# Cross attention of a decoder layer: weighings in pairs, other places for the maxima, the closing of the sums moved

## The reference, cut to what matters

```python
scores = jnp.einsum('bhqd,bhkd->bhqk', q, k) / np.sqrt(DK).astype(np.float32)
scores = jnp.where(mask == 0, jnp.float32(-1000000000.0), scores)
attn = jax.nn.softmax(scores, axis=-1)
out = jnp.einsum('bhqk,bhkd->bhqd', attn, v)
```

## Time and profile before

| | us |
|---|---|
| median of 3 runs | 3819.49 (3815.13 to 3820.21) |
| profiled execution | 3817.16 |
| its span, first to last instruction | 3815.3 |
| PE busy in the span | 3730.7 (98%) |
| granted share of PE's clock, mean | 0.993 |

### The profile page before, as it was taken

How to read it: one execution, slowest core, us unless ns; L and a number is a source line. 1 busy time by engine, 2 the same in 40 slices (tenths; PEclk the granted TensorE clock), 3 DMA queues, 4 the chain that set the end, 5 groups by cost and what they waited for, 6 DMA issues and landing times. The chain is left out here.

```text
span 3815.3 us, 62978 instructions
## 1 busy us (share of the span) xinstructions
PE 3730.7 (98%) x18664; PEld 2480.3 (65%) x18665; DVE 2386.6 (63%) x6129; ACT 1434.0 (38%) x1793; POOL 1687.6 (44%) x984
## 2 busy tenths in 40 slices
PE   8999999999988999999999999999999999999998
PEld 7888888788876544444444444454444777777886
DVE  6544444344466888888888888888888543434235
ACT  3222222222333455545555455545555221222332
POOL 2222222200023776677666766676665222312334
PEclk9999999999999999999999999999999999999999
DMA  6444444555565122222211222222211434327679
GB/s 203 125 128 131 134 121 121 162 199 187 180 196 180 36 58 58 58 56 58 58 29 34 58 58 59 58 56 58 48 31 40 157 123 138 111 89 257 213 279 340
DMA packets 245485, 446.75 MB, mean 117 GB/s; under 512 B 20024, under 2 KB 104536, under 8 KB 241244
## 3 DMA queue, kind: packets, MB, share of 16 engines
q1 hardware_dynamic: 215196, 366.37, 33.3%
q0 software_dynamic: 14752, 49.29, 3.6%
q10 hardware_dynamic: 15264, 27.79, 1.9%
HBM read 262.21 MB, written 181.17 MB: 116 GB/s over the span
## 5 line engine op out<-in xcount | busy, mean ns | idle before, releaser
L1165 DVE CUSTOM_DVE_ANT_0 xf_unread<-xa_mx_ps,mask_q 128x402 bf16<-128x402 f32 x1984 | 1033.7, 574 | 279.0 <-PE xa_mx_ps L1158 152.8
L1788 ACT ACTIVATE probs<-xa_scores 128x1024 f32<-128x1024 f32 (+1 forms) x416 | 417.5, 1024 | 417.6 <-PE xa_scores L1662 411.5
L1788 ACT ACTIVATE xa_probs<-xa_scores 128x1024 f32<-128x1024 f32 (+1 forms) x416 | 417.3, 1024 | 387.0 <-PE xa_scores L1662 387.0
L1662 PE MATMUL xa_scores<-mask_t,ident_b 128*128 128x512 bf16 (+1 forms) x1664 | 549.4, 388 | 0.0
L1623 POOL TENSOR_TENSOR xa_sums<-xa_sums,xa_probs 128x1024 f32<-128x1024 f32 x220 | 519.6, 2383 | 18.1 <-POOL xa_sums L1623 15.9
L1623 POOL TENSOR_TENSOR xa_sums<-xa_sums,probs 128x1024 f32<-128x1024 f32 x220 | 519.4, 2380 | 18.1 <-POOL xa_sums L1623 14.6
L1158 PE MATMUL xa_mx_ps<-xa_kp,queries 96*128 96x402 f32 x1024 | 364.7, 418 | 0.0
L1158 PE MATMUL xa_mx_ps<-xf_kp,queries 96*128 96x402 f32 x960 | 342.1, 418 | 0.0
L1656 PE MATMUL xa_scores<-queries,xf_kp 97*128 97x512 f32 (+1 forms) x832 | 284.7, 423 | 15.1 <-ACTq L1810 8.3
L1158 PEld LDWEIGHTS xa_mx_ps<-xa_kp,queries 96*128 96x128 f32 x1024 | 181.7, 189 | 169.4 <-DVE xf_maxima L1165 107.8
L1656 PE MATMUL xa_scores<-queries,xa_kp 97*128 97x512 f32 (+1 forms) x832 | 284.5, 423 | 1.8 <-ACT probs L1788 1.8
(11 more groups left out here) (418 smaller groups left out, 7258.4 us busy)
## 6 DMA issues: line engine op xcount, KB each, us to landing
turned_p<-rows SPq DMA_DIRECT2D x31, 1024.0 KB, 3.8
rows<-turned_p SPq DMA_DIRECT2D x124, 256.0 KB, 4.6
bridge_rows<-sorted_in SPq DMA_DIRECT2D x78, 256.0 KB, 3.3
sorted_out<-ex_made ACTq DMA_DIRECT2D x78, 256.0 KB, 4.3
queries<-qT_high SPq DMA_DIRECT2D x30, 512.0 KB
xf_kp<-kT_high SPq DMA_DIRECT2D x16, 800.5 KB, 11.8
xa_kp<-kT_high SPq DMA_DIRECT2D x16, 800.5 KB
rows<-in_ctx SPq DMA_DIRECT2D x16, 768.0 KB, 4.8
```

The source lines that it names most:

```text
L1165: return dve.tensor_tensor_reduce(out=unread[slot % 2][:, :], in0=scores[:, 0:MKEYS], in1=mask_q[:, half * QB + qt, MFIRST[kb]:MFIRST[kb] ...
L1662: last = pe.matmul(scores[pr][0:keys, jj, :], ident_b[0:keys, 0:keys], mask_t[0:keys, kt, queries], start=False, stop=True)
L1788: act.activation(prob[ring][pr][0:keys, :, :], scores[pr][0:keys, :, :], ACT.Exp, scale=SCALE).then_inc(exped, 1)
```

## The change

PE weighs in pairs: tiles 0 and 1 in step 1, 2 and 3 in step 3, and so on, and tiles 10, 11 and 12 in step 11 (`WEIGHED_AT`). The slots go to steps 10, 11, 12 (three, three, two of the unit after the next one), then to steps 0 to 8 as 2, 7, 5, 8, 6, 8, 6, 8, 6. Their banks are written out in `BANKS`; up to slot 11 only banks 0 and 2 take turns, but for slot 0. `add_up` moves to step 0 of the next unit, and ACT's copy of the total (`keep_sum`) with it. DVE adds four tiles (8 to 11) and POOL eight instead of nine. DVE reads slots 0 to 2 before it adds tile 9, slots 3 to 5 before tile 10, and slots 6 and 7 before tile 11. The inversion becomes a transpose, a reciprocal on 16 columns and a transpose back, and these three and the multiplication go before the readings of slots 14, 17, 19 and 23. All engines' loops run over eight units instead of four; those of PE and ACT become `later_loops` too.

```diff
-    SLOTS_OF = [2, 7, 8, 8, 8, 8, 8, 8, 7] + [0] * (KT - 9)
-    SLOT_OF = [sum(SLOTS_OF[:n]) for n in range(KT + 1)]
-    assert SLOT_OF[KT] == SLOTS
+    SLOTS_AT = {10: 3, 11: 3, 12: 2, 0: 2, 1: 7, 2: 5, 3: 8, 4: 6, 5: 8, 6: 6, 7: 8, 8: 6}
+    EARLY = (10, 11, 12)
+    SLOTS_OF, first_slot = {}, 0
+    for kt, count in SLOTS_AT.items():
+        SLOTS_OF[kt] = range(first_slot, first_slot + count)
+        first_slot += count
+    assert first_slot == SLOTS
+    AHEAD = SLOTS_OF[EARLY[-1]].stop
+    BANKS = [1, 2, 0, 2, 0, 2, 0, 2, 0, 2]
+    BANKS += [(0, 2, 1)[n % 3] for n in range(SLOTS - len(BANKS))]
+    SUM_BANK = 1
+    BEFORE_SUMS = max(n for n in range(AHEAD) if BANKS[n] == SUM_BANK)
+    AFTER_SUMS = min(n for n in range(AHEAD, SLOTS) if BANKS[n] == SUM_BANK)
+    AFTER_PEAKS = BANKS.index(0)
     TURN = 9
-    OWN = {"pool": tuple(range(9)), "dve": (9, 10, 11)}
+    WEIGHED_AT = {1: (0, 1), 3: (2, 3), 5: (4, 5), 7: (6, 7), 9: (8, 9), 11: (10, 11, 12)}
+    INVERSION = {4: 0, 7: 1, 9: 2, 13: 3}
+    OWN = {"pool": tuple(range(8)), "dve": (8, 9, 10, 11)}
...
                     m = SLOTS * u + slot
-                    pe.wait_ge(mx_read, m + 2)
-                    scores_of_slot(pe, mx_ps[slot % 3], qp[par], kp[par], half, slot).then_inc(mx_made, 1)
+                    back = next(n for n in range(1, SLOTS) if BANKS[slot - n] == BANKS[slot])
+                    pe.wait_ge(mx_read, m - back + 5)
+                    scores_of_slot(pe, mx_ps[BANKS[slot]], qp[par], kp[par], half, slot).then_inc(mx_made, 1)
...
-                def weigh(u, par, kt, ring):
+                def weigh(u, par, kt, ring, ahead):
                     keys = keys_of(kt)
                     if kt == 0:
                         pe.wait_ge(o_kept, u + 2)
                     pe.wait_ge(exped, PAIRS * (KT * u + kt + 1) + 1 + PAIRS)
                     if kt == KT - 1:
                         pe.wait_ge(sum_kept, u + 2)
+                        if ahead:
+                            pe.wait_ge(mx_read, SLOTS * (u + 2) + BEFORE_SUMS + 5)
                         four_heads(sum_ps, lambda mine: ones[0:keys, :], prob[ring], True, False)
...
                 def unit(u, par, half, at, more):
                     nxt = (par if half == 0 else 1 - par, 1 - half)
+                    first = isinstance(u, int) and u == 0
+                    ahead = more and not (isinstance(u, int) and u == units - 2)
                     for kt in range(KT):
-                        slots = iter(range(SLOT_OF[kt], SLOT_OF[kt + 1]) if more else ())
+                        early = kt in EARLY
+                        slots = iter(SLOTS_OF.get(kt, ()) if (ahead if early else more) else ())
+                        if first and kt == 0:
+                            slots = iter(range(AHEAD + len(SLOTS_OF[0])))
 
                         def maxima(most):
                             for slot in itertools.islice(slots, most):
-                                mx(u + 1, *nxt, slot)
-
+                                if early and slot == AFTER_PEAKS:
+                                    pe.wait_ge(row_kept, u + 4)
+                                if slot == AFTER_SUMS:
+                                    pe.wait_ge(sum_kept, u + 2)
+                                if early:
+                                    mx(u + 2, 1 - par, half, slot)
+                                else:
+                                    mx(u + 1, *nxt, slot)
+
+                        if ahead and kt == EARLY[0] and half == 0:
+                            pe.wait_ge(loaded, 16 * (LOADS * (u // HALF + 1)))
                         following = (u, par, half, kt + 1) if kt + 1 < KT else (u + 1, *nxt, 0) if more else None
-                        between = 1 if kt else 0
                         for pr in range(PAIRS) if following else ():
                             score(*following, pr)
                             if pr == 1:
-                                maxima(between)
+                                maxima(1)
                             add_mask(following[2], following[3], pr, 0)
-                            if pr == 0:
-                                maxima(between)
+                            maxima(1)
                             add_mask(following[2], following[3], pr, 1)
                             if pr == 0:
-                                maxima(between)
+                                maxima(1)
                         if more and kt == TURN:
                             turn_peaks(u + 1)
-                        maxima(2 * between)
-                        weigh(u, par, kt, (at + kt) % RING)
-                        if more and kt == 0:
-                            pe.wait_ge(row_kept, u + 3)
-                            pe.wait_ge(sum_kept, u + 2)
-                            if half == 1:
-                                pe.wait_ge(loaded, 16 * (LOADS * (u // HALF + 1)))
-                        maxima(SLOTS_OF[kt])
+                        maxima(2)
+                        if kt == 0 and not first:
+                            add_up(u - 1, OWN)
+                        for due in WEIGHED_AT.get(kt, ()):
+                            weigh(u, par, due, (at + due) % RING, ahead)
+                        maxima(SLOTS)
...
-                    add_up(u, OWN if more else OWN_LAST)
+                    if not more:
+                        add_up(u, OWN_LAST)
...
+                def keep_sum(u, half):
+                    act.wait_ge(total_made, u + 3)
+                    act.activation(sum_sb[half][:, :], sum_ps[:, :], ACT.Copy).then_inc(sum_kept, 1)
...
+                        if kt == 0 and not (isinstance(u, int) and u == 0):
+                            keep_sum(u - 1, 1 - half)
...
+                def invert(u, half, part):
+                    mine = sum_sb[half]
+                    if part == 0:
+                        dve.wait_ge(sum_kept, u + 3)
+                        dve.transpose(mine[:, :], mine[:, :]).then_inc(inverted, 1)
+                    elif part == 1:
+                        dve.wait_ge(inverted, 3 * u + 1 + 3)
+                        dve.reciprocal(inverse[:, :], mine[:, 0:BANK:DK]).then_inc(inverted, 1)
+                    elif part == 2:
+                        dve.wait_ge(inverted, 3 * u + 2 + 3)
+                        dve.transpose(mine[:, :].rearrange("p (c d) -> p c d", d=DK),
+                                      inverse[:, :].unsqueeze(2).broadcast_to([P, BANK // DK, DK])).then_inc(inverted, 1)
+                    else:
+                        dve.wait_ge(inverted, 3 * u + 3 + 3)
+                        dve.wait_ge(o_kept, u + 3)
+                        dve.wait_ge(stored, 16 * (u + 2))
+                        dve.tensor_tensor(out[:, :], o_sb[half][:, :], mine[:, :], ALU.mult).then_inc(finished, 1)
+
                 def finish(u, half):
-                    dve.wait_ge(sum_kept, u + 3)
-                    dve.reciprocal(sum_sb[half][:, :], sum_sb[half][:, :]).then_inc(inverted, 1)
-                    dve.wait_ge(inverted, u + 3)
-                    dve.wait_ge(o_kept, u + 3)
-                    dve.wait_ge(stored, 16 * (u + 2))
-                    dve.tensor_tensor(out[:, :], o_sb[half][:, :], sum_sb[half][:, :], ALU.mult).then_inc(finished, 1)
+                    for part in range(4):
+                        invert(u, half, part)
...
+                    first = isinstance(u, int) and u == 0
+                    ahead = not (isinstance(u, int) and u == units - 2)
+                    for slot in range(0 if first else AHEAD, SLOTS):
+                        if slot - SLOTS_OF[1].start in INVERSION and not first:
+                            invert(u - 1, 1 - half, INVERSION[slot - SLOTS_OF[1].start])
                         read(u + 1, 1 - half, slot)
-                    if more:
-                        peak(u + 1)
-                        for i, kt in enumerate(OWN["dve"]):
-                            for pr in range(PAIRS):
-                                add(u, kt, (at + kt) % RING, i, pr, POOL_ADDS)
-                    if not (isinstance(u, int) and u == 0):
-                        finish(u - 1, 1 - half)
+                    peak(u + 1)
+                    for i, kt in enumerate(OWN["dve"]):
+                        for slot in SLOTS_OF[kt + 1] if ahead and kt + 1 in EARLY else ():
+                            read(u + 2, half, slot)
+                        for pr in range(PAIRS):
+                            add(u, kt, (at + kt) % RING, i, pr, POOL_ADDS)
...
```

More of the change, by code:

```diff
@@ L1487, in cross_attention @@
         ones = sb("ones", [P, DK])
+        inverse = sb("inverse", [P, BANK // DK])
         unread, maxima, neg_max, max_row = first.unread, first.maxima, first.neg_max, first.max_row
@@ L1494, in cross_attention @@
         mx_ps = [ps(f"mx_ps{i}", [P, BANK]) for i in range(3)]
-        peak_ps, sum_ps = mx_ps[0], mx_ps[1]
+        peak_ps, sum_ps = mx_ps[0], mx_ps[SUM_BANK]
```

(40 more changed lines are left out.)

## The result

The kernel after takes 3984.62 us (3974.83 to 3987.95, 5 runs) against 3819.49 us (3815.13 to 3820.21, 5 runs) before: a ratio of 1.043 [1.0418, 1.0443], slower by 165 us. The forecast was 3870. The sign was right, the size was not, and the time lies outside the range. The execution profiled takes 3984.48 us (span 3982.7).

A forecast was written before the change was run, and what follows sets the result against it. PE's stream of matmuls was taken to bound the kernel. Savings and waits summed to +1.85 us for each of units 1 to 29, ends +5, loops -5: +53 on 3817.2, so 3870 us, range 3838 to 3898.

The forecast's parts named there:

- The inversion: Steps 1 to 3: its parts between DVE's readings, multiplication 0.69 as before, delay slots 26 and 27; cost 1.35 us a unit.
- my walk: Both engines followed from step 1's first score: steps 1 to 3 together take 14.9 us, 13.5 if the inversion costs nothing.
- The switches: Entering and leaving the array's strips at each weighing: 7 instead of 13 a unit, 0.317 each, saving 1.9 us a unit.
- slot 5: Step 11: waits for DVE's reading of slot 3 in the same bank, behind two additions; PE stands 1.63 us a unit.
- rival D: Inversion's transpose back costs up to 2.31 us, not 0.71; +48 at most, 3895 to 3918 us; chance 0.10.
- the pace: Steps 4 to 8: DVE's readings hold slots 35 and 41; 1.2 us a unit lost, against 0.6 before.
- the jumps: Loops of eight units: two jumps back instead of six, 1.31 us of idle PE each, -5.2 us in all.
- Rival B: Scores and masks pass a waiting slot, so PE isn't held; 51.2 us a unit, 3742 us; chance 0.06.
- Rival C: No change: only slot 5's wait is real, inversion lies in DVE's gaps; 53.5 us a unit, 3809 to 3817; chance 0.12.

The follow-up runs named there:

- a2: The changed kernel with slots 0 to 5 on three banks in turn, the multiplication left in place: 3944.71 us, ratio 1.0286 to the kernel before.
- a3: The changed kernel with the inversion's multiplication moved behind the reduction of the maxima and slots 0 to 5 on three banks: 3829.79 us, ratio 0.9988 to the kernel before.
- a4: The changed kernel with all four parts of the inversion behind the reduction of the maxima and three banks: 3821.73 us, ratio 0.9968 to the kernel before.
- a7: a3 plus an unused one-operand reciprocal of 384 constant columns ahead of slot 23's reading, once a unit: 3925.89 us, ratio 1.0277 to the kernel before.
- b1: The kernel before plus one unused DVE multiplication per unit, 512 columns, both operands in SBUF, ahead of slot 23's reading: 3938.72 us (+103).
- a1: The changed kernel with only the inversion's multiplication moved behind the reduction of the maxima: 3901.06 us, ratio 1.0166 to the kernel before.
- c1: The kernel before with only the weighings in pairs, slots as before: 3943.55 us, ratio 1.0287 to the kernel before.
- c3: The kernel before with the weighings in pairs and loops of eight units: 3892.65 us, ratio 1.0198 to the kernel before.

## Why the prediction was wrong

Of the 3.85 us a unit that are missing between 55.49 and 59.34:

- **The step that failed is "The inversion"**, where it says "the multiplication of 0.69 as before". It is 2.51 at its new place. From the first score of step 1 to that of step 4 my walk had 14.9 us; the units that run these steps at full clock take 16.4 to 16.8. That is some 1.8 a unit, 53 us in all. The held multiplication alone costs 3.79 - 1.48 = 2.31 of waiting (a2 to a3). The walk was wrong in two smaller things, of opposite sign: the transposes and the reciprocal cost 0.2 a unit (a3 to a4) and not the 0.95 that it gave the transposes, and with no part of the inversion in it (a4) the block takes 14.0, not 13.5. I took over a duration from a place where POOL was idle into one where my own account had POOL adding ("34.3" us of pairs from step 0 on), and asked only when DVE is free. The Trainium skill, SBUF — State Buffer, Who interferes with whom, says that a Vector instruction with two SBUF inputs contends with a GpSimd instruction that reads SBUF, that the port pair they share is an exclusive lock, and that the order of issue decides who blocks. The runs agree: 2.51 and 2.14 with two inputs in SBUF, 0.71, 0.25 and 2.55, the times without POOL, with one. And the trace of before had a row for it, in the last unit, where it starts 2.06 us into an addition of POOL's and ends 0.55 behind it:

```profile
2911.98 0.86 DVE L1848 TENSOR_TENSOR any_key<-xa_o_sb,xa_sum_sb 128x512 f32<-128x512 f32 x1
```

- **The clock was in no step.** I added waits to an engine that had stood at full clock for 1670 us, and priced each wait at its length. 112.6 us at half clock cost 56, 1.9 a unit, more than either wait was thought to cost. That a wait brings this was shown by a7, b1 and the pairs a1, a3 and a2, a3.
- The remaining 0.2 a unit I haven't traced. The switches, at 0.27 instead of 0.317, are 0.3 a unit by themselves.

What held: slot 5 (1.55 for 1.63, and gone with three banks); the price of a switch, nearly (0.27 for 0.317); the durations of the transposes and the reciprocal, so that rival D is out; the pace (0.5 a pair of steps); the jumps (6 to 7 us for 5.2). Rival B is out by the gaps. Rival C is out: the inversion cost 2.5 a unit of waiting, not nothing, and the steps that were to show it took 16.4 or more, not 13.5. In total: 3870 + 53 + 56 is 3979 of the 3985.

## What to carry to other kernels

When an instruction moves to another place of its engine, look up what the other engines do at that place: if it reads two operands in SBUF and POOL's additions run there, price it at the rest of POOL's instruction plus 0.55 us (its own time alone is 0.69). When a wait is put into a stream of matmuls that never stood, add a second term for the clock: about half of the wait here (0.62 for 1.55, 1.42 for 2.3, 1.9 for the two together). And measure a good part (here the pairs, -1.6 a unit) in the version with the bad parts out; put alone into the old layout it looked like a loss.

## What the runs showed of the hardware

- In a1 the starts of two matmuls of PE lie 1.74 us apart once a unit, and 11 of the 30 units have a stretch at 1.2 GHz behind it. With 2.53 (a7) it is 24 of 30, with 4.6 to 6.6 (c1 and c3) 8 of 8. The kernel before has six such gaps at its jumps, 1.5 to 1.9 from start to start, and none has one. So these runs give no length at which the clock falls.
- POOL pays as well: its addition that begins while the held multiplication works is 2.81 instead of 2.36.
- A jump of ACT's took up to 8 us in c1 and c3. The timeline shows no wait; the DMA packets show one of instructions that started 4.1 to 5.4 us after ACT's last copy, and ACT going on 1.8 to 1.9 us after its end.
- An instruction of DVE with both operands in SBUF, begun while one of POOL's ran, ended 0.55 us behind it in all 30 units and in 30 of b1; with one operand in PSUM the same operation kept its 0.69.
